# A one-core decoder layer: the turned keys of the cross attention are loaded during the query tiles, quarter by quarter of the heads, and the next context tiles are requested at step 10

## The reference

```python
x = x + attn(layernorm(x), W_qkv, W_out, b_out)            # 16 heads, rotary, window of 128
x = x + xattn(layernorm(x), ctx, Wq, Wk, Wv)               # 32 heads of 16
x = x + moe(layernorm(x), router, gate_proj, up_proj, down_proj)   # 64 experts, top 8

def xattn(x, context, Wq, Wk, Wv):
    q = x @ Wq.T
    kv = concat([context @ Wk.T, context @ Wv.T], -1).reshape(b, m, 32, 16, 2)
    k, v = kv[..., 0], kv[..., 1]                          # per head
    q, k = rmsnorm(q), rmsnorm(k)
    return softmax(q @ k.T * 16 ** -0.5) @ v
```

## Time and profile before

| | |
|---|---|
| median of 3 executions | 1841.28 us (1836.23 to 1843.69) |
| the profiled execution | 1848.08 us, of which the span from first to last instruction 1846.3 us |
| PE busy | 1448.3 us, 78% |
| DVE, ACT, POOL busy | 1055.3, 991.3, 774.7 us |
| granted TensorE clock, mean | 0.902 |
| cross attention, walk | about 512 to 1166 us of the span |

### The profile page before, as it was taken

One profiled execution on the slowest core, in us unless ns is written; L12 is line 12 of the kernel. 1 busy time (PEld: TensorE's weight loads), 2 busy tenths in 40 slices (PEclk: granted clock), 3 DMA queues, 4 the chain that ended last, 5 costly groups with the idle time before them and its releaser, 6 DMA issues. The chain is left out here.

```text
span 1846.3 us, 28824 instructions
## 1 busy us (share of the span) xinstructions
PE 1448.3 (78%) x9682; PEld 1075.2 (58%) x9682; DVE 1055.3 (57%) x1863; ACT 991.3 (54%) x1952; POOL 774.7 (42%) x485
## 2 busy tenths in 40 slices
PE   3898888899856198588858879426899999999990
PEld 2677676777644044244324423316788889989990
DVE  4766575776536034134223432478688888888880
ACT  3555454555422066445635668104677777777770
POOL 2444343443430045134424500020476777767772
PEclk9998999999979599789979989555899999999996
DMA  5000000000021831850581192240799999999986
GB/s 203 1 24 12 24 12 24 12 24 18 12 89 57 143 63 47 134 140 24 99 152 58 46 137 58 95 163 15 219 291 272 277 291 293 300 274 284 293 191 120
DMA packets 132769, 230.51 MB, mean 125 GB/s; under 512 B 17657, under 2 KB 50681, under 8 KB 132160
## 3 DMA queue, kind: packets, MB, share of 16 engines
q1 hardware_dynamic: 102848, 155.70, 31.1%
q0 software_dynamic: 29248, 72.53, 18.0%
q10 hardware_dynamic: 576, 0.98, 0.2%
HBM read 164.50 MB, written 71.83 MB: 128 GB/s over the span
## 5 line engine op out<-in xcount | busy, mean ns | idle before, releaser
L934 ACT ACTIVATE stage<-xa_ring 128x1024 f32<-128x1024 f32 x256 | 246.7, 1031 | 80.0 <-PE xa_ring L1200 79.9
L911 POOL TENSOR_TENSOR xa_power<-xa_ms,xa_half 128x32 f32<-128x32 f32 x24 | 130.3, 5428 | 323.0 <-DVE xa_ms L1041 323.0
L273 POOL TENSOR_TENSOR sa_prob<-sa_prob,sa_rinv 128x1024 f32<-128x1024 f32 x64 | 121.3, 1896 | 241.2 <-DVE sa_rinv L436 241.2
L1558 POOL DMA_INDIRECT ex_xg<-xn,token x128 | 160.4, 1253 | 102.3 <-DVE ex_y L1688 54.6
L331 ACT ACTIVATE sa_prob<-sa_sc_ps,sa_nmax 128x256 f32<-128x256 f32 x256 | 118.0, 473 | 110.6 <-DVE sa_nmax L423 110.6
L72 PE MATMUL ex_ba<-ex_xh,ex_wh 128*128 128x256 f32 x512 | 150.4, 294 | 16.6 <-issue 14.3
L73 PE MATMUL ex_ba<-ex_xl,ex_wh 128*128 128x256 f32 x512 | 145.6, 284 | 0.0
L74 PE MATMUL ex_ba<-ex_xh,ex_wl 128*128 128x256 f32 x512 | 145.6, 284 | 0.0
L1212 PE MATMUL xa_out<-stage,xa_v 128*17 128x512 f32 x1024 | 138.6, 614 | 0.6 <-ACT stage L934 0.4
L1659 DVE TENSOR_TENSOR ex_wl<-ew_raw,ex_wh 128x1024 fp32r<-128x1024 f32 (+1 forms) x128 | 117.2, 957 | 37.0 <-ACT ex_wh L1602 36.4
L423 DVE TENSOR_REDUCE sa_nmax<-sa_sc_ps 128x2 f32<-128x512 f32 x128 | 82.9, 687 | 65.4 <-PE sa_sc_ps L568 65.4
(11 more groups left out here) (243 smaller groups left out, 4147.3 us busy)
## 6 DMA issues: line engine op xcount, KB each, us to landing
ew_raw<-in_L_ffn_gate_proj_dram SPq DMA_DIRECT2D x64, 384.0 KB
ew_raw<-in_L_ffn_up_proj_dram SPq DMA_DIRECT2D x64, 384.0 KB
turned<-stage SPq DMA_DIRECT2D x64, 256.0 KB, 2.8
ew_rawd<-in_L_ffn_down_proj_dram SPq DMA_DIRECT2D x64, 256.0 KB
xa_kT<-turned SPq DMA_DIRECT2D x96, 128.0 KB, 8.4
xa_qT<-turned SPq DMA_DIRECT2D x96, 128.0 KB, 10.8
ew_rawd<-in_L_ffn_down_proj_dram SPq DMA_DIRECT2D x64, 128.0 KB
sa_x<-in_x_dram SPq DMA_DIRECT2D x16, 256.0 KB, 2.7
```

Source lines behind the costliest of these rows:

```text
L273: pool.tensor_tensor(prob[:, 4 * g:4 * g + 4, :], prob[:, 4 * g:4 * g + 4, :], rinv[:, 4 * g:4 * g + 4].unsqueeze(2).to_broadcast([P, 4, 2 ...
L911: pool.tensor_tensor(power[:, i], ms[:, i], half[:], ALU.pow).then_inc(s_pw, 1)
L934: act.activation(prob[:, w % 2, 2 * i:2 * i + 2, :], ring[i][:], ACT.Exp, scale=D2 ** -0.5).then_inc(s_ex[i], 1)
L1558: pool.indirect_dma_start(out=xg[:, e % RING, j, :], out_offset=None, in_=xn3, in_offset=bass.IndirectOffsetOnAxis(token[:, at:at + 1], 0))\
```

## The change

`load_turned` gets a third argument: side 0 loads the 6 DMAs of the keys of a quarter, side 1 the 6 of the queries. Side 0 waits only for the stores of the four key tiles (`32 * (n * KQ + 4)`), side 1 for all eight as before. The keys of quarters 0 and 1 are loaded one step after the last key tile is stored (step 17; w = -16 for batch 0), ahead of the stores of the query tiles in SP's queue. The queries of quarters 0 and 1 and both sides of quarter 2 stay at step 26 (w = -9), and quarter 3 stays at step 0. No DMA is added or dropped: 48 loads for each batch. `load_context` of tiles 0 and 1 of the next batch is issued two steps after the last context tile of the batch before it is turned: at step 10 in place of 24 and 28, and at w = -22 in place of -8 and -4 for batch 1.

```diff
-            def load_turned(n, q):
-                sp.wait_ge(st_h, 32 * (n + 1) * KQ)
+            def load_turned(n, q, side):
+                sp.wait_ge(st_h, 32 * (n * KQ + T * (side + 1)))
                 if n > 0:
                     for i in range(2):
                         sp.wait_ge(s_sc[i], STEPS * (n - 1) + 2 * T * (q + 1))
-                for side, where in enumerate((kT, qT)):
-                    rows = turned[n % 2, side].rearrange("a (pair i d) t -> a i d pair t", i=2, d=D2)
+                rows = turned[n % 2, side].rearrange("a (pair i d) t -> a i d pair t", i=2, d=D2)
+                for r, part in enumerate(((0, 1, 0), (0, 0, 1))[side]):
                     for i in range(2):
-                        for r, part in enumerate((0, 1, 0) if side == 0 else (0, 0, 1)):
-                            at_row = i * W2 + r * D2
-                            sp.dma_start(where[at_row:at_row + D2, 4 * q:4 * q + 4, :].bitcast(F32),
-                                         rows[part, i, :, 4 * q:4 * q + 4, :]).then_inc(ld_h[q], 16)
+                        at_row = i * W2 + r * D2
+                        sp.dma_start((kT, qT)[side][at_row:at_row + D2, 4 * q:4 * q + 4, :].bitcast(F32),
+                                     rows[part, i, :, 4 * q:4 * q + 4, :]).then_inc(ld_h[q], 16)
...
-                for n, t in at(lambda n, t: x_step(n, t) - 4, w, [(n, t) for n in range(1, B) for t in range(2)]):
+                for n, t in at(lambda n, t: x_step(n - 1, T - 1) + 2, w, [(n, t) for n in range(1, B) for t in range(2)]):
                     load_context(n, t)
...
                 for n in range(B):
+                    if w == kn_step(n, T - 1) + 1:
+                        load_turned(n, 0, 0)
+                        load_turned(n, 1, 0)
                     if w == kn_step(n, KQ - 1):
-                        for q in range(3):
-                            load_turned(n, q)
+                        for q, side in ((0, 1), (1, 1), (2, 0), (2, 1)):
+                            load_turned(n, q, side)
                     if w == STEPS * n:
-                        load_turned(n, 3)
+                        for side in range(2):
+                            load_turned(n, 3, side)
```

## The result

The changed kernel takes 1752.76 us (1743.64 to 1757.24, 4 runs) against 1842.49 us before (1836.23 to 1844.23, 4 runs): a ratio of 0.9513, with the 95% interval 0.9466 to 0.9559. The gain is 90 us where 77 were forecast; 1764 was predicted, and 1752.76 lies 0.8 us inside the lower end of the range (1752 to 1785).

What follows compares the result with a forecast made beforehand. PE's waits for DMAs queued on SP were taken as the bound; 28.5 + 22.5 + 22.9 + 5.5 + 2.8 + 1.0 - 1.5 - 4 - 1 = 76.7 us gained gave 1764 us, range 1752 to 1785.

Steps and rivals of the forecast that it cites:

- The six waits: PE's waits for context and turned tiles before batch 0 and at the first steps of batches 1 to 3: 92.4 us.
- Context request: Request at step 10 removes waits of 19.87 and 19.73 us in batches 1 and 2, plus 2.8 us of low clock.
- Early keys in batch 0: Batch 0: key loads delay the query stores, query loads start at 612.8 instead of 608.82; scores still gain 28.5 us.
- Early keys later on: Batches 1 to 3: 0.5 us delay per key window; waits of 2.65 and 3.16 us go, 5.5 in batch 3.
- What is late next: With the stalls gone, ACT's copy into `hl` waits 2 us in batches 1 and 2; 1 us in batch 0's window.
- my unit: Time on the DMA engines for one 128 KB load of turned tiles: 0.846 us.
- slow case: Loads at 0.93 us per 128 KB; ACT's copy in batches 1 and 2 would then wait 6.5 us each.
- Two signs of being wrong: Wrong if PE waits at steps 4 or 8 for a hidden transfer; the first rival right if DVE waits for x tiles.
- the first rival: Late landings in the DMA queue all at the slow rate: 59 us gained, 1782, or 45 us and 1796; chance 0.20.
- the forecast's own case: Whole kernel at 1764 us, 77 us gained, with 1755 to 1776 as its own range; chance 0.70.
- the rival with fast loads: Query loads at less than half the expected time, nothing given back: 93 us gained, 1748 us; chance 0.05.
- the queue takes a good part back: Same as the first rival: late landings in SP's queue leave 59 us gained, 1782 us; chance 0.20.

Runs made afterwards that it cites:

- e1: The kernel before with only the context tiles requested earlier, turned tiles loaded as before: 1787.32 us, ratio 0.968.
- e2: The changed kernel with the context request put back, so only the keys are loaded earlier: 1808.23 us, ratio 0.98.
- e3: The changed kernel without early keys in batch 0, their loads issued with the queries: 1747.65 us in one execution.
- e10: The changed kernel again, unaltered: 1751.07 us.
- e9: The changed kernel, but batch 0 loads only quarter 0's keys early and quarter 2 later, quarter 3 at step 4 in each batch: 1744.83 us, ratio 0.9463.
- e8: The kernel before again, unaltered: 1841.31 us.
- e11: The kernel before again, unaltered, for a third trace: 1852.12 us.
- e5: The changed kernel, but batch 0 loads the keys of all four quarters early, 24 loads instead of 12: 1760.67 us in one execution.
- e0: The changed kernel again, unaltered: 1755.35 us, ratio 0.9496.

## Why the prediction was right, and where its size was off

**What bounds, and why: right.** The six waits were on the path, and the order of SP's queue made them. e1 and e2 each take away the part that the argument gave them, at the places it named.

**Context request: right.** In the first traces the stretch from batch 1's first scores to batch 2's fell from 156.2 to 131.1 us, 25.1; the steps of the sum gave 19.87 + 3.16 + 1.4 - 0.5 - 2 = 21.9. Most of the difference is the 2 us that were not given back.

**Early keys in batch 0: right in kind, a little too cheap.** The copy at the second query tile was to start 4.8 us late; from the turn of the first context tile it started 65.3 us on where it was 60.4, 4.9 late (the idle time before it was 6.53, 4.92, 4.42 and 3.99 us in the four traces). The query loads went out 5.4 us later than before, 4 were forecast, and the first scores came 26.9 us earlier, 28.5 were forecast. "Pay for themselves and no more" is borne out by e1, the comparison that the prediction makes: it has no early keys and the same first scores (88.3). Beside e3, where the key loads are issued with the queries but don't wait for the last store, the early keys cost up to 2.6 us, a part of it the rate of that execution. That the key loads could start before the last store has landed is a gain that the sum has no term for; how much it is worth, one execution of e3 doesn't settle.

**Early keys later on: better than forecast.** No copy at step 21 waited. In batch 3 2.17 us stayed, 2.8 were forecast.

**What is late next: the place right, the price too high.** SP did stand at `load_x`, from the end of the row at 753.74 to 769.87, 13.5 us, in these rows of the changed kernel:

```profile
749.71 3.07 SPq L859 DMA_DIRECT2D out_dram<-xa_xs  x4
753.74 2.56 SPq L863 DMA_DIRECT2D xn<-xa_xn  x1
769.87 0.34 SPq L831 DMA_DIRECT2D xa_xs<-x  x1
770.26 0.98 SPq L842 DMA_DIRECT2D turned<-stage  x2
```

I let the key store behind it land 2 us after the copy at step 8 was due. In this trace it was issued at 770.26 and had landed when the copy started at 775.70; in e10 that copy waited 0.17 us. What was wrong in the term is the one price for all bytes: 0.846 us for 128 KB, so 1.69 us for each transfer of 256 KB. Behind 24 loads of `turned`, issued from 730.01 on, came two context tiles, twelve loads and the four result stores. By their order and their bytes they fall into these windows of the changed kernel:

```profile
742.00:754.00 12.00, 12.00 (x69) 6.11 (x69) 7.44 (x19) 7.90 (x12) 7.65 (x4) 1.00 1.09 132
755.50:757.00 1.50, 0.63 (x8) 0.39 (x4) 0.87 (x2) 1.29 (x2) 0.00 (x0) 1.00 1.04 346
758.00:768.00 10.00, 8.50 (x46) 4.69 (x45) 5.83 (x12) 4.38 (x7) 3.57 (x1) 0.83 1.09 138
768.50:771.00 2.50, 2.50 (x18) 1.48 (x18) 0.00 (x0) 1.65 (x4) 2.42 (x2) 1.00 1.05 396
```

The loads took 0.95 to 0.99 us for 128 KB, more than my unit, and by the "slow case" of the prediction the copy should have waited 6.5 us. It didn't, since the context tiles and the result stores took only about 0.7 us for 256 KB. (The sum of the prediction also counts 2.0 us of latency here where it has 2.8 elsewhere, and the 146 GB/s in its comparison with the Trainium skill belong to none of its rows; the twelve loads of the slow case give 142.)

DVE's waits for the x tiles, up to 5.2 us (6.1 in e10), were hidden: e9, which has none, is no faster from the first scores of batch 1 to those of batch 2. In place of it the third context tile of batch 1 was late, by 2.44, 2.14 and 2.85 us in three of the four traces (in e10 it was in time). It stands behind 24 loads issued from 617.24, and these passed at 133 GB/s from 625 to 639, 0.99 us each. At 0.846 they would have ended about 3 us sooner, before PE came. I had put 1 us into the sum for this window.

**Two signs of being wrong did come.** The prediction called itself wrong if a transfer that it calls hidden is waited for at steps 4 or 8: the third context tile of batch 1 at step 4 of batch 0 is that case, at a price of 2 to 3 us. And it gave the first rival the case if DVE waits for the x tiles. DVE did, and yet the queue took nothing back, so that sign was badly chosen: here a wait of DVE was not one of PE.

**The size: the sum fits its trace, the trace was a short one.** From the first pair of traces the cross attention gained 80.3 us, forecast 76.7. The mean of three traces of before less the mean of four of the changed kernel is 770.9 - 681.2 = 89.7 us, and that is the measured 90. Of the 13 us between 76.7 and 89.7, 8.0 are the first trace's cross attention below the mean of the three. Of these, 5.2 are the term that was mis-sized, the 92.4 us of waits, taken from one execution in which the DMA engines ran at 162 GB/s: in two others the same waits were 96.8 and 103.7 us. The rest goes with the clock: PE was busy 523.7 us in the cross attention of the first trace, 527.0 in e8's and 530.5 in e11's; from batch 2's first scores to batch 3's the granted clock was 0.87 in the first trace and 0.82 in e11. The changed kernel differs less between executions (677 to 684 us); that fewer of its bytes are waited for is a likely reason. My sentence that the profiled execution lies 6.8 us above the median and "the gain is the same in both" hid this: its expert phase was 15 us long, and its cross attention below the other two. Some twenty of its experts took about 8.4 us instead of 7.57: from 1300 to 1800 us PE stood 14.3 us in 20 gaps before L72, for nothing that the profile names, and e8 has none of them, at the same mean clock of the phase (0.96). The cause is open; it was not seen again in thirteen traces.

**The range: held by luck in part.** 1752.76 lies 0.8 us above its lower end; of the later medians of the same kernel 1755.35 lies inside, 1750.22 and 1751.07 outside. It lies outside the 1755 to 1776 of the forecast's own case, and nearer to the 1748 of the rival with fast loads than to 1764, though that rival's mechanism did not occur.

**The rivals.** That the queue takes a good part back is what e5 makes happen on purpose, and not what the change does. The fast loads did not occur: in stretches of loads from `turned` alone the engines moved 129 (e0) to 163 GB/s (before). The 341 GB/s that the Trainium skill (DMA: Bandwidth & Descriptors, Measured) has for transfers of 1 MB are not reached by these loads, but by the context tiles and result stores of 256 KB in the same queue (346 and 396 GB/s in the windows above). So pieces of 2 KB, which the prediction named beside the low rate, can't be the reason alone: a row of a context tile is 2 KB too. What differs in the kernel's code is that a load fills 16 partitions and a context tile 128; whether that is the cause was not tried. By the Trainium skill (DMA: Bandwidth & Descriptors, Queues, rings and completion order) an engine takes descriptors in ring order; 12 and 24 early loads agree (first scores at 88.3 and 100.0 us).

## What to carry to other kernels

A DMA queue issued from one engine is a list in time: for each transfer, add up the time of what stands in front of it, and compare that with when it is needed, not with when it could first be sent. Add up by kind of transfer: here 128 KB took 0.8 to 1.0 us in one kind, and 256 KB about 0.7 us in another. A tile of 0.25 MB requested behind 4.7 MB cost 78 us in three places; the earlier request alone gave 52 (traces) to 60 us (medians) of gain, since it left the next tile behind the loads, and with the keys split off too 2.4 us of the 78 were left. An early load is free only if it fits the gap before the next store that someone waits for; past that it is paid in full, here from 12 loads to 24 (e5). And a stall on a DMA varies between executions with the rate: price it from more than one trace, or give the range for it.

## What the hardware showed that was not expected

The rate at which the 16 DMA engines passed the same loads, always at a share over 1, differed between executions of one kernel: 162, 155 and 134 GB/s in the three waits before batch 0. It can pass for an effect of an edit: a part of the 2.6 us by which e3's first scores lead is its rate, 155 GB/s beside 135 in e1.

The share of the DMA engines doesn't tell how fast they are. In one queue, within 30 us and at shares of 1.04 to 1.09, loads from `turned` passed at 132 to 138 GB/s, context tiles at 346 and result stores at 396. A mean over such a stretch (168 GB/s from 741 to 771 us) describes neither kind.
